# Four heads at a time in the linear-attention scan, and the first 768 rows of W2 loaded ahead

## The reference, cut to what matters

```
# layer 0, inner network: repeated 6 times, width 1024, inner width 2730
hg = xn @ W1 + b1                      # W1: 1024 x 5460
a, gate = split(hg, 2)
x = a * gelu(gate) @ W2 + b2 + x       # W2: 2730 x 1024

# layer 1, linear attention, 16 heads of 64, 64 features
phi_q = exp(q @ omega.T - |q|^2/2) / 8 ; phi_k likewise
kv_cumsum = cumsum(phi_k (x) v) ; k_cumsum = cumsum(phi_k)
out = (phi_q . kv_cumsum) / (phi_q . k_cumsum + 1e-6)
```

## Time and profile before

| | us |
|---|---|
| median of 2 runs | 36877.21 |
| the two runs | 36995.60 and 36758.83 |
| the profiled execution, device time | 36996.14 |
| its span on the slowest core (core 3) | 36993.8 |
| its spans on the other cores | 36464.5 to 36912.8 |
| TensorE busy (matmuls) | 19802.5 |
| VectorE busy | 9192.8 |
| stage F, first L1474 to the last copy | 2664.4 |

### The profile page before, as it was taken

One profiled execution on the slowest core, in us unless ns is written; L12 is line 12 of the kernel. 1 busy time (PEld: TensorE's weight loads), 2 busy tenths in 40 slices (PEclk: granted clock), 3 DMA queues, 4 the chain that ended last, 5 costly groups with the idle time before them and its releaser, 6 DMA issues.

```text
span 36993.8 us, 261181 instructions; the slowest of 8 cores (36464.5 to 36993.8 us)
## 1 busy us (share of the span) xinstructions
PE 19802.5 (54%) x86532; PEld 8156.6 (22%) x86532; DVE 9192.8 (25%) x16272; ACT 6304.0 (17%) x9424; POOL 2507.1 (7%) x1805
## 2 busy tenths in 40 slices
PE   2555554445754477444764467443774457124468
PEld 0010011222222222222222222221222222012234
DVE  2010011332223321333223322233212322244420
ACT  1333332111111100111111110111111110101112
POOL 0000000110001100110001100111001100000000
PEclk8555555556765577556765577555775567556679
DMA  2000000001210022001220022000220022230011
GB/s 59 4 5 4 4 4 16 16 16 28 48 44 16 15 50 54 16 16 26 48 46 15 16 43 50 28 16 24 48 47 16 16 33 52 99 106 7 7 40 47
DMA packets 1100254, 1146.07 MB, mean 31 GB/s; under 512 B 769476, under 2 KB 844366, under 8 KB 1093824
## 3 DMA queue, kind: packets, MB, share of 16 engines
q0 software_dynamic: 668096, 366.46, 6.9%
q1 hardware_dynamic: 430848, 762.91, 6.1%
HBM read 1076.14 MB, written 318.77 MB: 38 GB/s over the span
## 4 chain that ended last, share of the span: by engine, by line
PE 53%; DVE 16%; ACT 12%; issue 7%; DMA 6%; POOLq 3%; DVEq 1%; ACTq 0%; SPq 0%; another core or an unknown queue 0%; POOL 0%; PEldq 0%
PE pb L707 7%; PE pb L1050 6%; PE pb L1116 6%; PE pb L1055 6%; ACT arena L471 5%; ACT arena L846 5%; PE pb L482 4%; PE pb L462 3%; PE pb L836 3%; POOLq L117 3%; PE pb L910 3%; DMA arena<-r 3%; PE pb L869 2%; PE pb L1740 1%; PE pb L1776 1%
## 5 line engine op out<-in xcount | busy, mean ns | idle before, releaser
L1050 PE MATMUL pb<-arena 128*128 128x512 bf16 (+1 forms) x8448 | 3656.8, 433 | 81.1 <-DMA arena<-W 81.1
L1055 PE MATMUL pb<-arena 128*128 128x512 bf16 (+1 forms) x8448 | 3653.6, 432 | 0.0
L846 ACT ACTIVATE arena<-pb,arena 128x512 bf16<-128x512 f32 x2232 | 1734.5, 777 | 6144.7 <-PE pb L836 6144.7
L707 PE MATMUL pb<-arena 128*128 128x512 bf16 x9216 | 2569.9, 451 | 390.7 <-DVE arena L689 264.7
L482 PE MATMUL pb<-arena 128*17 128x512 bf16 x2304 | 1343.6, 583 | 2633.5 <-ACT arena L471 1836.3
L1116 PE MATMUL pb<-arena 128*128 128x512 bf16 (+1 forms) x8448 | 2273.4, 429 | 410.7 <-DMA arena<-W 410.7
L869 PE MATMUL pb<-arena 128*128 128x65 bf16 x8928 | 844.5, 236 | 3073.0 <-DVE arena L858 1193.8
L471 ACT ACTIVATE arena<-pb,arena 128x512 bf16<-128x512 f32 x2304 | 1790.3, 777 | 3947.0 <-PE pb L462 3947.0
L720 ACT CAST arena<-pb 128x512 bf16<-128x512 f32 x1152 | 675.3, 586 | 7312.4 <-DVE arena L733 4119.0
L1078 DVE TENSOR_TENSOR arena<-pb,arena 128x512 bf16<-128x512 f32 (+1 forms) x1056 | 730.2, 691 | 4510.4 <-ACT arena L1073 4510.4
L796 PE MATMUL pb<-arena 128*128 128x128 bf16 x1536 | 194.3, 307 | 2546.1 <-DVE arena L775 2546.1
(11 more groups left out here) (248 smaller groups left out, 20793.1 us busy)
## 6 DMA issues: line engine op xcount, KB each, us to landing
r<-arena SPq DMA_DIRECT2D x416, 512.0 KB, 2.9
arena<-r SPq DMA_DIRECT2D x416, 512.0 KB, 4.2
arena<-W POOLq DMA_DIRECT2D x504, 256.0 KB, 5.5
arena<-r SPq DMA_DIRECT2D x372, 256.0 KB, 2.9
arena<-W POOLq DMA_DIRECT2D x12, 5376.0 KB, 30.0
arena<-x SPq DMA_DIRECT2D x96, 512.0 KB, 4.6
arena<-Wqkv POOLq DMA_DIRECT2D x6, 6144.0 KB, 40.5
arena<-s SPq DMA_DIRECT2D x64, 512.0 KB, 5.5
```

The costliest lines, as they stand in the source:

```text
L707: ctx.op("tensor", lambda e, c=c, g=g, b=b, gb=gb, off=off: e.matmul(psum[gb][:, :], bufs["C_rT"][b][:, 129 * c + off:129 * c + off + 128] ...
L846: exp_toks[(g, ci)] = ctx.op("scalar", lambda e, ptb=ptb, sbank=sbank: e.activation(bufs["C_pt"][ptb], psum[sbank][:, :], AF.Exp, bias=cc[ ...
L1050: ctx.op("tensor", lambda e, c=c, ng=ng, js=js, jw=jw, ab=ab: e.matmul(psum[ab][0:jw, :], bufs["C_w1a"][js][:, 128 * c:128 * c + jw], bufs ...
L1055: ctx.op("tensor", lambda e, c=c, ng=ng, js=js, jw=jw, gb_=gb_: e.matmul(psum[gb_][0:jw, :], bufs["C_w1g"][js][:, 128 * c:128 * c + jw], b ...
```

## The change

Two edits that do not depend on each other.

The first is in stage C. W2's load is split. Its first 6 chunks (768 rows) are issued by GpSimd at the start of each half, into the first 6144 columns of `C_U`; the transposed tokens move behind them, to columns 6144 to 22528 (the buffer is exactly that long). The other 15 chunks and the last 42 rows are loaded where all of W2 was loaded before. TensorE's first W2 matmul waits for the early load and the last gelu product only; its seventh (j == 6) waits for the rest.

The second is in stage F. The head loop becomes a loop over 4 groups of 4 heads. The heads of a group are every other one (0, 2, 4, 6; then 8 to 14; then 1, 3, 5, 7; then 9 to 15), so that their features lie in the same half of the partitions. Each VectorE instruction now covers the four heads of a group in one PSUM bank.

```diff
@@ stage C
+            we2 = [("sT", ffn2_done)] if (half == 1 and ffn2_done) else []
+            ctx.op("gpsimd", lambda e, l=l: e.dma_start(
+                out=bufs["C_U"].rearrange("p (c x) -> p c x", c=22)[:, 0:6, :],
+                in_=io["W2"][l][0:768].rearrange("(c p) d -> p c d", p=128)),
+                waits=we2, inc="d7", inc_n=16)
+            w2_early = ctx.cnt["d7"]
...
-                    bufs["C_U"][:, 0:16384].rearrange("p (c x) -> p c x", c=8)[:, :, 128 * t:128 * t + 128],
+                    bufs["C_U"][:, 6144:22528].rearrange("p (c x) -> p c x", c=8)[:, :, 128 * t:128 * t + 128],
...
-                out=bufs["C_U"].rearrange("p (c x) -> p c x", c=22)[:, 0:21, :],
-                in_=io["W2"][l][0:2688].rearrange("(c p) d -> p c d", p=128)),
-                waits=[("sV", h_done)], inc="d7", inc_n=16)
+                out=bufs["C_U"].rearrange("p (c x) -> p c x", c=22)[:, 6:21, :],
+                in_=io["W2"][l][768:2688].rearrange("(c p) d -> p c d", p=128)),
+                waits=[("sV", h_done), ("d7", w2_early)], inc="d7", inc_n=16)
...
-                            wt.append(("d7", w2_tok))
+                            wt.append(("d7", w2_early))
...
+                        elif j == 6:
+                            wt.append(("d7", w2_tok))
@@ stage F
-        for h in range(16):
...
+        H0 = [0, 8, 1, 9]
+        for g in range(4):
+            h0 = H0[g]
...
+            mask_tok[g] = ctx.op("vector", lambda e, atb=atb, ab=ab: e.tensor_tensor(
+                bufs["F_AT"][atb], psum[ab][:, :], bufs["tri_up4_sb"], ALU.mult),
                 waits=wm, inc="sV", drain=True)
...
+            ctx.op("vector", lambda e: e.reciprocal(
+                bufs["F_z2"][:, 0:4].unsqueeze(2), bufs["F_z"][:, 0:4].unsqueeze(2)), drain=True)
...
         scan_done[i] = ctx.cnt["sT"]
+        all_norm = max(norm_tok.values())
         for c in range(8):
-            wt = [("sV", norm_tok[2 * c + 1]), ("sV", norm_tok[2 * c])]
+            wt = [("sV", all_norm)]
```

136 lines of the change are left out of this document (77 added, 59 removed).

## The result

| | before | changed |
|---|---|---|
| median, us | 36847.07 (10 runs) | 36145.46 (12 runs) |
| lowest and highest, us | 36693.62 to 36995.60 | 35943.37 to 36349.33 |
| ratio, 95% interval | | 0.9815 (0.9781 to 0.9849) |
| span of the profiled execution, us | 36993.8 (core 3) | 36239.9 (core 2) |

The changed kernel takes 702 us less. The forecast was 740 less. The interval contains 0.98, so whether it is faster by over 2% stays undecided.

A forecast was written before the change was run, and what follows sets the result against it. No engine bounds the whole program; stage F's head loop is a TensorE-VectorE handover ring, and W2's load a bandwidth wait. 717 + 120 - 97 = 740 us off the median 36877 gives 36140 us, 8-in-10 range 35990 to 36290.

The forecast's parts named there:

- its own case (715 to 790): Whole kernel: the forecast's own case, a saving of 715 to 790 us, given a chance of 0.48.
- The group, 4.30: Stage F head loop: one group of four heads costs 4.30 us, against 9.96 for four heads before.
- the alternative of 0.39 for the copy: Stage F group: the bf16 copy on 260 columns takes 0.39 us at 1.05 ns a column, instead of 0.30.
- "longer group" rival (4.7): Stage F: strides or wider matmul spacing make a group 4.7 us, saving 689, time 36190 us; chance 0.25.
- Stage F, 717: Stage F: the grouped head loop saves 717 us over 32 tiles.
- The saving is 22.4 us a tile: Stage F: a tile's head loop falls from 40.5 to 18.05 us, taken as the tile's whole saving.
- The bound of minus 95 us: Stage F: eight matmuls at L869's 0.05 spacing would shorten a group by 0.74 us, saving 95 us more.
- W2's gain, 120: Stage C: late load lands 8.6 us sooner, six early matmuls give 1.4; 10.0 us a half, 120 us.
- W2's price, 97: Stage C, start of a half: early load shares one DMA engine with the 127-row load; 8.0 us a half, 97 lost.
- The free early load: Start of a half: the early W2 load costs nothing, saving 837 us, time 36040 us; chance 0.17.
- that rival: Stage F head loop: TensorE's clock rises above 0.50, saving 68 us more, time 36070 us; chance 0.07.
- The hold-up that it would take to be slower: Start of a half: SyncE's loads starve beside the early load; kernel slower only from 70 us a half; chance 0.02.

The follow-up runs named there:

- e5: Changed kernel with each group's eight output matmuls ordered as four with 128-row weights, then four with 64-row weights, instead of alternating; median 35549.27 us, ratio 0.9817 to before.
- e3: Changed kernel with the early W2 load issued one tile later, behind the first tile's bf16 cast; median 35877.47 us, ratio 0.9817 to the kernel before.
- e4: Changed kernel with the first tile's 127-row load written as one of 112 rows and one of 15; median 35617.48 us, ratio 0.9793 to before.
- e9: Changed kernel with the edits of e3, e4 and e6, plus the late W2 load in four pieces, two tiles worked together; median 35114.21 us, ratio 0.9574 to before.
- e6: Changed kernel with the head loop software-pipelined, the next group's products and mask issued before the present normalisation; median 35386.29 us, ratio 0.9764 to before.

## Why the prediction was right, point by point

**The total.** 740 forecast, 702 measured between the medians. By the rows it is 696 + 18 = 714, and at one clock (36220 - 35633) / 0.81 = 725. Every term fell inside its bounds. All three are smaller than forecast, by 21, 10 and 5 us, and the last one offsets a part of the other two. The sum by the rows is at the lower edge of its own case (715 to 790). That the medians agree with it to 12 us is partly luck, since the executions of one kernel are spread over 300 to 400 us.

**The group, 4.30: measured 4.34.** Copy 0.29, scaling 0.42, state 0.42 and mask 0.69 fell where the wider rows of other stages put them; neither the strides nor the four segments cost anything extra. So the alternative of 0.39 for the copy and the "longer group" rival (4.7) are out. The eight matmuls stood 0.164 apart instead of 0.155, which makes 0.06, and the handovers around the copy gave 0.02 of it back.

**Stage F, 717: measured 696.** The saving is 21.7 us a tile, not 22.4. The loop itself saved the forecast 22.4: it took 18.3 us where the forecast was 18.05, but before it took 40.7 on average, where the one tile of the earlier trace rows has 40.5. The miss is a term that the sum did not have: the output projection behind the loop takes 0.6 us more a tile (0.2 in its first half and 0.4 in its second), as TensorE's clock rises 1.4 us later there. The step that failed is "The saving is 22.4 us a tile", which stopped at the loop's end. Why the clock rises later stays open.

**The bound of minus 95 us.** The prediction weighed the spacing of L869 (0.05) against that of the pair (0.155) and stayed with the pair, because its weights change shape. e5 shows that this reason was the right one (0.05 within one shape, 0.16 to 0.18 at each change), and that nearly the whole bound is to be had: 0.68 us a group by order alone, where it had 0.74.

**W2's gain, 120: measured 110.** 9.2 us a half instead of 10.0. The load lands in 22.7 instead of 21.4, 7.3 us sooner and not 8.6, so it isn't quite proportional to its bytes, as the lower bound (102) allowed. The other term was too small: the six early matmuls were priced at 0.23 us each, a rate of clock 0.97, but behind the wait TensorE stands at 0.50, and in the kernel before 2.5 us lie between the first and the seventh, not 1.4. So two misses of opposite sign nearly cancel, and that is luck: with the right sizes the sum would have been 7.3 + 2.5 = 9.8, of which 9.2 reach the first output sum.

**W2's price, 97: measured 92.** 7.6 us a half instead of 8.0. The 28.2 us that the sum divides stand in none of the rows; with the 30.0 of the earlier trace rows it would be 8.6, and the packets counted above give 7.9. e3 and e4 show that the two loads share one engine, that the price disappears when the early load comes later, and that 2.9 us a half of it are left when the 127 rows are spread. The packets of the two queues alternate one by one on that engine, 0.246 us a pair. That two loads on one engine delay each other by the whole of their packets was the author's assumption in the forecast: of the kernel before, the rows show the share of 0.06 and L658's 45.9 us, and not how two queues divide one engine.

**The rivals.** The free early load is out by the wait of 298.5 us. The clock stays at 0.50 in the loop, with TensorE 53% busy, so that rival is out too. The hold-up that it would take to be slower, 70 us a half, was 7.6.

**What the prediction passed over.** It priced the 127-row load as something that the early load would collide with. That this load alone costs every half of the kernel before 9 us (206.8 us of wait against 94.3 in e9) could be guessed in the earlier trace rows already, from the share of 0.06.

## What to carry to other kernels

When two engines hand work back and forth, a few wide steps in place of many narrow ones can shorten the ring (9.96 to 4.34 us for four heads), but the ring stays; here issuing the next group's products and mask ahead of the present group's normalisation took its waits out (4.34 to 2.86). Price a prefetch by what runs on the engines that it uses at that moment: moving it by one tile turned an edit worth 20 us into one worth 110. Cutting the 127-row transfer beside it into 112 and 15 rows gained 170 us, of which some 110 had nothing to do with the prefetch. Group matmuls by the shape of their weights: each change of shape cost 0.1 us here. Where the granted clock moves the totals by 1%, read an edit from the waits and durations of its stage, and compare totals at one clock.

## What the runs showed of the hardware

- In the kernel before, a transfer of 127 rows of 2 KB ran alone at 25 GB/s with a DMA share of 0.06, one engine of 16, and made one update of its semaphore. As 112 and 15 rows it made 31, and the 15-row piece landed in 7.4 us at the median beside the early load (e4).
- On one engine the packets of the two queues alternated one by one: 0.246 us a pair (changed kernel, core 2, 9560 to 9561), where the rows of the one queue alone came 0.081 apart (9564 to 9570).
- The early load landed in 16.8 us at the median beside the 127-row load (changed, L954), in 14.9 beside 112 and 15 rows (e4, L954) and in 11.1 one tile later (e3, L1009). SyncE's next issue (L966, the slowest core of the changed kernel) took 9.7 to 11.7 us beside it in the second halves of the six layers and 4.3 to 14.9 in the first halves, where it took 2.8 to 4.0 and 4.6 to 7.1 before (L959), and 0.4 to 1.4 in e4 (L966).
- At clock 0.50, matmuls whose weights alternate between 128 and 64 rows started 0.164 us apart (changed, L1634 and L1637), those of one shape 0.05 apart in the same place (e5, L1634 and L1640, 65 columns).
- The mean granted clock of a core went with its span: 41.5 to 46.8 us for each 0.001 in the kernels here, with a scatter of 24 to 39 us (spans and clocks of all executions). The levels behind the mean were 0.50, 0.81 and 1.00, and 128x512 matmuls started 0.427, 0.263 and 0.216 us apart at them (changed, core 2).
- The clock rose at different times in the output projection, by the clock records counted from its first matmul and averaged over the tiles of one core (core 0 before and changed, core 1 in e5 and e6): 4.2 us before, 5.6 changed, 4.2 in e5, 3.9 in e6. Neither the length of the loop ahead of it (40.7, 18.3, 15.6 and 13.1 us) nor how busy TensorE was in it (31% before, 53% changed) orders these four. Why it is so was not tried. Neither was the reason for the q, k, v projections at 0.81 in some tiles of some cores (cores 2 and 3 of the changed kernel, cores 6 and 7 of the one before).
